# Gated memory: scatters in one run, and a new order of VectorE's gated output and normed output

## The reference, cut to what matters

```python
def step(carry, inp):
    M, n, m = carry
    qt, kt, vt, li, lf, op = inp
    m_next = jnp.maximum(lf + m, li)
    i_s = jnp.exp(li - m_next)
    f_s = jnp.exp(lf + m - m_next)
    M = f_s[:, :, None] * M + i_s[:, :, None] * (vt[:, :, None] * kt[:, None, :])
    n = f_s * n + i_s * kt
    h_raw = jnp.einsum('bij,bj->bi', M, qt)
    denom = jnp.maximum(jnp.abs(jnp.einsum('bi,bi->b', n, qt))[:, None], 1e-06)
    h = jax.nn.sigmoid(op) * (h_raw / denom)
    return ((M, n, m_next), h)
...
out = out / sqrt(mean(out * out) + 1e-08) * norm_scale        # and h = h + out
...
logits = layernorm(h) @ gate_w + gate_b                       # the router of the experts
idx = argmax(softmax(logits))                                 # one expert for each token
buf = zeros((E, C, D)).at[idx, pos].set(x)                    # tokens sorted by expert
```

## Time and profile before

| | us |
|---|---|
| median of 3 runs | 3207.94 (3207.86 to 3208.52) |
| the profiled execution | 3205.61 |
| its span in the trace | 3203.7 |

### The profile page before, as it was taken

How to read it: one execution, slowest core, us unless ns; L and a number is a source line. 1 busy time by engine, 2 the same in 40 slices (tenths; PEclk the granted TensorE clock), 3 DMA queues, 4 the chain that set the end, 5 groups by cost and what they waited for, 6 DMA issues and landing times. The chain is left out here.

```text
span 3203.7 us, 68709 instructions
## 1 busy us (share of the span) xinstructions
PE 2828.8 (88%) x25818; PEld 1557.7 (49%) x25818; DVE 2414.1 (75%) x3224; ACT 2182.1 (68%) x3138; POOL 1916.0 (60%) x1191
## 2 busy tenths in 40 slices
PE   7999999969999999995599958899999999999997
PEld 5666666635555555553244413344444444444444
DVE  6888888858888888884387637777777777777783
ACT  6777777758887888872244447677777777777762
POOL 8888888811677777777200066666666666666530
PEclk9999999989999999996799969999999999999999
DMA  1111111111221221211444421111212211212111
GB/s 48 42 42 39 42 40 42 39 59 37 61 72 54 73 60 51 62 43 51 145 149 151 137 61 35 36 54 46 58 52 52 56 52 53 56 49 55 47 35 49
DMA packets 208269, 191.21 MB, mean 60 GB/s; under 512 B 76381, under 2 KB 163398, under 8 KB 207562
## 3 DMA queue, kind: packets, MB, share of 16 engines
q1 hardware_dynamic: 173850, 142.95, 15.4%
q0 software_dynamic: 25600, 26.01, 3.3%
q10 hardware_dynamic: 8496, 17.87, 1.5%
HBM read 99.08 MB, written 87.65 MB: 58 GB/s over the span
## 5 line engine op out<-in xcount | busy, mean ns | idle before, releaser
L2428 POOL TENSOR_TENSOR E_w<-E_w,E_rs 128x1024 f32<-128x1024 f32 x200 | 408.9, 2044 | 406.5 <-DVE E_rs L2336 406.5
L2421 POOL DMA_INDIRECT E_row<-yb,P_gi x400 | 388.4, 971 | 395.4 <-POOLq L93 301.6
L689 POOL DMA_INDIRECT xb<-B_yt,P_gi x400 | 469.0, 1172 | 115.4 <-issue 113.9
L204 POOL TENSOR_TENSOR A_kmask<-A_ksb,A_pack_a 128x3584 f32<-128x3584 f32 x56 | 356.2, 6361 | 115.3 <-ACT A_ksb L374 115.3
L2220 ACT ACTIVATE E_w<-E_w 128x1024 f32<-128x1024 f32 x200 | 211.6, 1058 | 241.0 <-DVE E_w L2329 241.0
L2333 DVE TENSOR_REDUCE E_sm<-E_w 128x16 f32<-128x1024 f32 x200 | 243.8, 1219 | 127.0 <-ACT E_w L2220 125.2
L2321 DVE TENSOR_REDUCE E_mx<-E_lg 128x16 f32<-128x1024 f32 x200 | 242.1, 1210 | 114.8 <-PE E_lg L1985 113.9
L474 DVE COPY A_vbd<-A_v 128x512 f32<-128x512 f32 x336 | 215.6, 684 | 74.3 <-PE A_v L324 74.3
L2329 DVE TENSOR_TENSOR E_w<-E_lg,E_mx 128x1024 f32<-128x1024 f32 x200 | 244.7, 1223 | 6.4
L2016 PEld LDWEIGHTS E_wt<-S_pack_f,E_w 128*128 128x128 f32 (+1 forms) x1600 | 169.6, 141 | 159.1 <-issue 132.6
L1985 PE MATMUL E_lg<-S_wxs,E_yo 64*128 64x512 f32 x800 | 228.0, 646 | 7.6 <-DVE E_w L2329 7.4
(11 more groups left out here) (321 smaller groups left out, 6803.3 us busy)
## 6 DMA issues: line engine op xcount, KB each, us to landing
R_xs<-xb SPq DMA_DIRECT2D x57, 256.0 KB, 2.7
yb<-R_ys SPq DMA_DIRECT2D x57, 256.0 KB, 2.0
B_x<-h SPq DMA_DIRECT2D x25, 512.0 KB, 4.0
h<-B_hh SPq DMA_DIRECT2D x25, 512.0 KB, 3.2
A_xg<-in_xw SPq DMA_DIRECT2D x56, 224.0 KB, 2.5
h<-A_res ACTq DMA_DIRECT2D x56, 224.0 KB, 2.5
E_hx<-h SPq DMA_DIRECT2D x48, 256.0 KB, 2.6
out<-E_ob SPq DMA_DIRECT2D x96, 128.0 KB
```

The costliest lines, as they stand in the source:

```text
L204: nc.gpsimd.tensor_tensor(kmask[i % 2][:], bc(ksb[i % 2][:].unsqueeze(2), [128, J, H, Q]), bc(head_of_row[:].unsqueeze(1).unsqueeze(3), [1 ...
L689: pool.indirect_dma_start(out=xb, out_offset=bass.IndirectOffsetOnAxis(ap=routed.gi[0:k, c, b:b + 1], axis=0), in_=yt[c % LT][0:k, D * row ...
L2421: pool.indirect_dma_start(out=row[b % LR][:, k, i], out_offset=None, in_=yb, in_offset=bass.IndirectOffsetOnAxis(ap=idx[:, c, 2 * n + i:2 ...
L2428: TT(w3, w3, bc(rs[g % 3][:].unsqueeze(2), [128, 2 * SH, G]), ALU.mult).then_inc(w_done, 1)
```

## The change

VectorE: `normed_out(t-2)` moves from the end of the turn to a place right behind `norm_query(t-1)`, ahead of `forget_middle`. `outputs` moves from the start of turn `t + 1` to the end of turn `t`, ahead of `forget_sum`. `slots` and `numbers` of chunk `t - 4` move ahead of `norm_sum`. `residual` itself stays where it was.

GpSimd: all 16 scatters of a chunk stand in one run behind `scale_memory`, and they are those of chunk `t - 4` where they were those of `t - 5`.

```diff
--- before.py
+++ after.py
@@ -693,10 +693,9 @@
 
                 for t in range(CHUNKS + 5):
                     at(weigh_keys, t - 1)
-                    at(scatter, t - 5, range(0, 5))
                     at(age_memory, t - 2)
                     at(scale_memory, t - 1)
-                    at(scatter, t - 5, range(5, B))
+                    at(scatter, t - 4, range(B))
                 for u in range(LT):
                     pool.wait_ge(sent[u], 16 * B * len(range(u, CHUNKS, LT)))
 
@@ -1358,7 +1357,6 @@
                        bc(rtemp.unsqueeze(2), [K1, SH, G]), ALU.mult).then_inc(wxp_done, 1)
 
                 for t in range(CHUNKS + 4):
-                    at(outputs, t - 2)
                     at(ends, t - 1)
                     at(exponents, t - 1)
                     at(first_max, t - 1)
@@ -1381,17 +1379,18 @@
                     at(ranked, t - 4)
                     at(first_norm, t - 1)
                     at(own, t - 4)
+                    at(slots, t - 4)
+                    at(numbers, t - 4)
                     at(norm_sum, t - 1)
-                    at(slots, t - 4)
                     at(gate_out, t - 1)
-                    at(numbers, t - 4)
                     at(norm_weight, t - 1)
+                    at(norm_query, t - 1)
+                    at(normed_out, t - 2)
                     at(forget_middle, t)
-                    at(norm_query, t - 1)
+                    at(outputs, t - 1)
                     at(forget_sum, t)
                     at(last_max, t - 1)
                     at(last_norm, t - 1)
-                    at(normed_out, t - 2)
                 plan()
                 slices()
```

## The result

The change takes 3254.65 us (median of 4 runs, 3252.08 to 3257.12) against 3207.9 for the kernel before: ratio 1.014, 95% interval 1.0128 to 1.0153. It is slower by 46.7 us, where I had said 23. The profiled execution took 3257.12 us (span 3254.9) and is the slowest of the four.

What follows compares the result with a forecast made beforehand. A ring of VectorE and TensorE waits, 30.57 us a turn, was taken to bound the kernel. Turns +36, early turns −6, end −7 gave +23 on 3205.6: 3229, as median 3231 us; forecast 3214 to 3248 (0.62), wider range 3186 to 3252.

Steps and rivals of the forecast that it cites:

- the new ring: Gated memory: indices, scatters, scaled memory and TensorE's way to rms close over two turns, 64.7 us, 32.4 a turn.
- the indices to the next scatter: GpSimd: from the indices being ready to the first scatter of the run, 0.15 us.
- scaled memory to the next R: TensorE: from the scaled memory being ready to the next start of rms, 0.3 + 14.6 = 14.9 us.
- Stretch of the scatters: GpSimd: scatters held up by VectorE's two-input instructions, 6.0 us a chunk, bounds 3.9 and 7.5.
- Collision with the short steps: GpSimd's late products hold up VectorE's eight short steps; indices come 18.8 us behind the start of rms, not 15.15.
- Turns: Turns 5 to 25 of the gated memory: 20 × (32.4 − 30.57) = +36 us.
- Turns 2 to 4: Early turns have no late keys and gain at most 2.4 us each: −6 with the start of turn 5.
- The end: From the start of rms in turn 25 to the last scatter: 104.1 us in place of 110.8, so −7.
- rival 1: Products don't hold VectorE's short steps up much: 30.5 us a turn, 3190 us; chance 0.17.
- rival 2: The stretch of the scatters doesn't grow or vanishes: 3141 us; chance 0.03.
- Rival 3: VectorE becomes the ring, indices later than 20 us behind rms delay normed_out: turn 33.5, 3254 us; chance 0.08.
- Rival 4: Gains and collisions cancel: a turn of 31.2 us, total 3208 us; chance 0.10.

Runs made afterwards that it cites:

- e3: The change, plus three idle TensorE products ahead of turn_memory's wait for the scaled memory; 3259.59 us, ratio 1.0166.
- e5: The change, with place, ranked, own, slots and numbers of chunk t - 4 moved ahead of causal on VectorE; 3281.64 us, ratio 1.0231.
- e6: As e5, with aging and scaling of the memory moved from GpSimd to VectorE, ahead of residual; 3285.16 us, ratio 1.0242.
- e8: The change, with aging and scaling of the memory moved to VectorE, the indices where the change has them; 3220.18 us, ratio 1.0038.
- e9: As e8, with the run of sixteen scatters of chunk t - 5 in place of t - 4; 3188.52 us, ratio 0.9936.
- e10: As e8, with the weighted keys also made by VectorE, so that GpSimd has only scatters; 3181.76 us, ratio 0.9916.
- e12: The change, with eight small GpSimd fills of an own tile behind each run of sixteen scatters; 3299.76 us, ratio 1.0288.
- e1: The kernel before with VectorE's new order alone, the scatters as before; 3209.74 us, ratio 1.0009.
- e4: The change, with the run of sixteen scatters of chunk t - 5 in place of t - 4; 3220.51 us, ratio 1.0043.

## Why the prediction was wrong

The direction, the place and the collision of GpSimd's products with the short steps were as forecast. The time lay 2.65 us above the range of 3186 to 3252 (6.65 above the 3248 of the forecast itself), and the loss was twice what I gave. **The step that failed is the sum of the new ring, 64.7 us in two turns: above all its term "scaled memory to the next R", 14.9 us, which measured 16.45, and the 0.15 us from the indices to the next scatter, which measured 0.80.** That this ring over two turns is what sets the turn is not borne out either, as told below. The five terms on the mean of turns 8 to 23 are 67.4, two turns of 33.7:

| term | predicted | measured |
|---|---|---|
| R to indices | 18.8 | 19.1 |
| indices to the first scatter | 0.15 | 0.80 |
| run of sixteen, up to the keys | 26.15 | 26.5 |
| keys, aging, scaling | 4.7 | 4.5 |
| scaled memory to the next R | 14.9 | 16.45 |

- **Scaled memory to R.** The largest error. I took TensorE's steps at the length they had without a wait. I had predicted a 4 us wait, and did not ask what TensorE's clock does behind it: granted clock 0.52 in the turn shown. In the three turns in which `turn_memory` and `variance_out` both ran at full length this way took 14.8 us, as predicted. In e3 this way is 1.05 us shorter, and that is worth 0.4 us a turn.
- **Indices to the scatter.** I took the 0.15 us from between two instructions of GpSimd. After a wait it is 0.80.
- **Stretch of the scatters.** Predicted 6.0 us a chunk, measured 6.4 (21.9 of scatters less 16 x 0.97). The first of a run takes 2.33 us, not the 2.9 that I named as a sign. The two rows that I had shown for the stretch (1.98 and 2.95) lie beside scans. A TENSOR_TENSOR does it too: the scatter at 1027.09 meets `normed` (R+6.8 to R+8.0), takes 1.26 and ends 0.85 behind it.
- **Collision with the short steps.** Right: keys predicted at R+12.4 to 12.7, measured at 12.7; indices 18.8, measured 19.1; scaled memory 17.5, measured 17.2.
- **Turns.** +36 predicted, +60 measured. The 20 turns, each taken 1.25 us too short (32.4 against 33.65), are 25; the 2 us that I let stand take 2 off.
- **Turns 2 to 4.** -6 predicted, -3.2 measured. Turns 2 and 3 began 0.7 us later; only turns 3 and 4 were shorter, by 1.6 and 2.4.
- **The end.** -7 predicted, -4.3 measured.
- **Rivals.** The products do hold up the short steps (against rival 1), and the scatters are held up more than before (against rival 2). Rival 3 named the right size, 3254, by luck and for a wrong reason: VectorE stands 1.8 us ahead of `outputs` until `attend` has ended (1013.73), so it is not the ring. Rival 4's turn of 31.2 is far from 33.65.

What I did not see is theory C's ring of one turn: 0.8 + 26.5 + 4.5 + 1.9 (scaling's end to the indices) = 33.7. That this sum gives the turn proves nothing, and neither does 67.4 for two turns: each goes round between the same instructions, once or twice, and gives the measured turn whatever sets it. More is said by what releases what. In 16 of the turns 5 to 24 the indices come 1.9 to 2.0 us behind the end of the scaling, whether the keys started at R+11.4 or at R+12.7; in the other four (keys at R+14.0) they come 1.3 behind it. So in most turns GpSimd's products hold the indices back, and not the way from `rms`. By the two-turn ring e5, e6 and e8 should have been 80, 120 and at least 20 us faster than they were; e9 and e10 came out as theory C had them, and e12 did not.

The trace has a third tie, which neither theory has. In all 20 turns the scatter that meets the scan of `running_max` (1022.43, 1022.64) ends at R+6.0, 0.8 behind the scan, and the ones behind it follow at fixed places. So the keys start 4, 5 or 6 scatters later, at R+11.4 (3 turns), R+12.7 (13) or R+14.0 (4), and never in between. With the scaled memory 4.5 behind the keys' start and the next `rms` 14.8 to 17.5 behind that, this too closes within one turn. It shows why e3 gained so little: over the turns 5 to 24 the way to `rms` is 1.0 us shorter there, but the keys start at R+14.0 in 12 turns in place of 4, 0.6 us later on the mean. Which of these ties sets the turn of the change as it stands stays open.

A second thing that I had wrong, hidden in this change, is the gain that VectorE's new order should bring. e1 shows none: TensorE is freed, but GpSimd had only 2.0 us a turn to give (1.47 ahead of the keys and 0.53 ahead of the aging), and longer scatters took it (21.6 us a chunk against 19.4).

## What to carry to other kernels

When work is moved on an engine that is nearly full, write down where each of its other instructions lands in the turn, and what it will run beside; then close every ring that comes up, over one turn and over two, with the wait at both ends. A sum that gives the turn is no proof of its ring; an edit that shortens one term is. A wait for a value of the same turn was free when nothing waited back (e10), and cost 2.8 us a turn when products behind it held up those who make the value (the change against e4). And an engine that is given a new wait may not run behind it as it ran without it (`variance_out`, 3.67 us against 1.98).

## What the runs showed of the hardware

- A VectorE instruction with two inputs in SBUF stood until GpSimd's product was over, and it did not get in between two products that followed at once: `equals` took 3.50 us, across the keys and the aging.
- A scatter that had waited for its indices began 0.80 us behind them, against 0.15 to 0.30 behind another GpSimd instruction.
- A scatter that started while VectorE ran an instruction with two inputs in SBUF ended 0.8 us behind that instruction; one that started at another time took 0.97, also where such an instruction began later. By these two figures the lengths of 397 of the change's 400 scatters come out within 0.12 us.
- TensorE's granted clock was 0.52 in the 5.6 us behind a 3.5 us wait in turn 10, and 1.00 behind a wait as long in turn 13. `turn_memory` and `variance_out` kept their full length in 3 of 20 turns of the change, and in 13 of 20 with three idle products in that wait. The Trainium skill (TensorE: Matmul & The Clock Gate, § HAM oscillation — how this bites in real kernels) tells that TensorE drops to the lower clock when it idles between groups of matmuls; the trace agrees with it in turn 10, by that 0.52, and shows with turn 13 that it need not happen.
